# An attention step's order on three engines: key/value projection in three parts, output product behind two heads' scores

## What is computed

```
# attention, for each batch: 32 query heads in 8 groups that share a key/value head, D = 128
q = rope(rmsnorm(x @ Wq.T));  k = rope(rmsnorm(x @ Wk.T));  v = x @ Wv.T
k_all = concat(k_cache[pages], k);  v_all = concat(v_cache[pages], v)      # 512 cached + 128 new keys
probs = softmax(where(valid, q @ k_all.T / sqrt(D), -1e30))
attn  = (probs @ v_all) @ Wo.T
# then
s  = silu(attn @ Wgate.T);  the half of each row of s with the smallest |s| is set to 0
x1 = x + (s * (attn @ Wup.T)) @ Wdown.T
y  = x1 @ W_adapter[id].T;  out = x1 + y @ W_int4.T + b
```

## Time and profile before

| | |
|---|---|
| median of 3 runs | 1438.7 us (1435.5 to 1439.25) |
| the profiled execution | 1440.7 us, span from first to last instruction 1438.9 us |
| TensorE matmul busy | 1397.8 us, 97% |
| TensorE weight load busy | 1167.6 us, 81% |
| VectorE busy | 1178.5 us, 82% |
| ScalarE busy | 871.3 us, 61% |
| GpSimd busy | 803.4 us, 56% |
| mean granted TensorE clock | 0.998 |

### The profile page before, as it was taken

The page is one execution under the profiler, slowest core; times in us unless marked ns, Lnnn a source line. Parts: engine busy times, 40 slices in busy tenths (PEclk is TensorE's granted clock), DMA queues, the critical chain, the costliest instruction groups (busy, mean ns, idle before and its releaser), DMA issues.

```text
span 1438.9 us, 22830 instructions
## 1 busy us (share of the span) xinstructions
PE 1397.8 (97%) x7750; PEld 1167.6 (81%) x7750; DVE 1178.5 (82%) x2596; ACT 871.3 (61%) x2221; POOL 803.4 (56%) x822
## 2 busy tenths in 40 slices
PE   5899999999999999999999999999999999999998
PEld 4788888888888888888888888888888787666766
DVE  7888888888888889888988898889889977666662
ACT  6567666766676767666766676667667751332221
POOL 6566666666666666666666666666666621122211
PEclk9999999999999999999999999999999999999999
DMA  6111211121112111211121111111121303111111
GB/s 221 51 30 29 74 59 32 31 74 59 32 31 74 57 34 30 76 58 32 30 74 60 31 36 68 59 30 52 48 69 32 107 19 116 45 56 62 44 59 52
DMA packets 26767, 80.41 MB, mean 56 GB/s; under 512 B 9522, under 2 KB 10546, under 8 KB 23186
## 3 DMA queue, kind: packets, MB, share of 16 engines
q1 hardware_dynamic: 10258, 45.29, 8.9%
q0 software_dynamic: 16384, 33.59, 8.2%
HBM read 76.74 MB, written 2.10 MB: 55 GB/s over the span
## 4 chain that ended last, share of the span: by engine, by line
PE 86%; DVE 10%; issue 1%; ACT 1%; another core or an unknown queue 0%; DMA 0%; SPq 0%; POOL 0%; DVEq 0%; ACTq 0%
PE proj_ps L108 10%; PE proj_ps L110 9%; PE proj_ps L109 9%; PE turn_ps L712 8%; PE value_ps L108 5%; PE score_ps L108 5%; PE out_ps L877 5%; PE value_ps L110 5%; PE value_ps L109 5%; PE score_ps L110 4%; PE score_ps L109 4%; PE gu_ps L110 3%; PE gu_ps L108 3%; PE gu_ps L109 3%; DVE probs L1437 2%; DVE pt_lo L1462 2%
## 5 line engine op out<-in xcount | busy, mean ns | idle before, releaser
L515 POOL DMA_INDIRECT kg<-kc,idx x256 | 290.1, 1133 | 261.5 <-issue 254.1
L1122 ACT ACTIVATE pt_hi<-turn_ps 128x512 fp32r<-128x512 f32 x320 | 190.2, 595 | 210.2 <-PE turn_ps L712 171.2
L525 POOL DMA_INDIRECT vg<-vc,idx x256 | 251.2, 981 | 109.6 <-issue 58.9
L1462 DVE TENSOR_TENSOR pt_lo<-turn_ps,pt_hi 128x512 fp32r<-128x512 f32 x320 | 218.9, 686 | 66.5 <-ACT pt_hi L1122 49.3
L1116 ACT ACTIVATE probs<-probs,shift,rstd 128x640 f32<-128x640 f32 x256 | 234.0, 916 | 35.4 <-DVE shift L1426 35.4
L1437 DVE CUSTOM_DVE_ANT_0 probs<-score_ps,mask 128x640 f32<-128x640 f32 x256 | 205.4, 817 | 20.2 <-PE score_ps L110 17.9
L108 PE MATMUL proj_ps<-w_hi,xt_hi 128*128 128x512 f32 (+1 forms) x512 | 184.6, 361 | 13.6 <-DVE w_lo L1358 9.8
L712 PE MATMUL turn_ps<-cst,probs 128*128 128x128 f32 x1280 | 191.8, 272 | 0.0
L712 PEld LDWEIGHTS turn_ps<-cst,probs 128*128 128x128 f32 x1280 | 159.8, 140 | 26.4
L108 PE MATMUL score_ps<-kt_hi,qt_hi 128*128 128x320 f32 x512 | 165.1, 323 | 10.5 <-DVE qt_lo L1414 4.4
L110 PE MATMUL proj_ps<-w_hi,xt_lo 128*128 128x512 f32 (+1 forms) x512 | 174.6, 341 | 0.0
(11 more groups left out here) (197 smaller groups left out, 3191.9 us busy)
## 6 DMA issues: line engine op xcount, KB each, us to landing
w_raw<-wqkv SPq DMA_DIRECT2D x7, 1536.0 KB
wo_raw<-wo SPq DMA_DIRECT2D x8, 1024.0 KB
wa_sb<-wa SPq DMA_DIRECT2D x7, 1024.0 KB, 4.9
kg<-kc,idx POOLq DMA_INDIRECT x256
vg<-vc,idx POOLq DMA_INDIRECT x256
wg_raw<-wg SPq DMA_DIRECT2D x2, 1376.0 KB, 5.8
wu_raw<-wu SPq DMA_DIRECT2D x1, 2752.0 KB
wd_sb<-wd SPq DMA_DIRECT2D x1, 2560.0 KB, 9.7
```

The lines of the kernel that those rows point to most:

```text
L515: pool.indirect_dma_start(kg[:, b % 2, c, :], None, kc, bass.IndirectOffsetOnAxis(ap=idx[:, b * NC + c:b * NC + c + 1], axis=0))\
L525: pool.indirect_dma_start(vg[:, b % 2, c, :], None, vc, bass.IndirectOffsetOnAxis(ap=idx[:, b * NC + c:b * NC + c + 1], axis=0))\
L1122: act.activation(pt_hi[:, (b + j) % 2, :], turn_ps[1 - j % 2][:, :], ACT.Copy)\
L1462: dve.tensor_tensor(pt_lo[:, at, :], turn_ps[1 - j % 2][:, :], pt_hi[:, at, :].bitcast(F32), ALU.subtract).then_inc(p_lo_done[j], 1)
```

## The change

The work is the same; the order of the queues of TensorE, ScalarE and VectorE is another.

- TensorE: `project_kv` takes a list of chunks and is called three times: chunk 0 behind the turn of the cached keys, chunk 1 behind the last product with the values, chunks 2 and 3 behind the turn of the new keys. `turn_q` is between the first of them and `values(s, b, 4)`. `values(s, b, 3)` comes behind the last piece of `project_q`. `project_o` comes behind the scores of heads 0 and 1.
- ScalarE: `split_q` and `split_new_k` come before `split_o` and the copies of keys and values; the exponential of head 0 comes before chunk 0 of the next probabilities, from step 0 on.
- VectorE: `split_q` and `split_new_k` come directly behind `split_cached_k`, before `split_o`. The maxima of heads 0 and 1 come before the rotation of the queries and `add_up`. The division of head 0 comes before chunk 3.
- First steps: all eight masks are written before step -2 (before: three there, five in steps 0 to 4). In step -1 the rotation of step 2 and `split_x(4)` come before the maxima. `split_x(3)` goes behind the maxima of step -2.

```diff
-                    def project_kv(s, b, g):
-                        if b == 0:
-                            wait(pe, w_lo_done[2], g + 1)
-                        wait(pe, q_copied, s + 1)
-                        for k in range(NK):
+                    def project_kv(s, b, g, ks):
+                        if ks[0] == 0:
+                            if b == 0:
+                                wait(pe, w_lo_done[2], g + 1)
+                            wait(pe, q_copied, s + 1)
+                        for k in ks:
...
-                        last.then_inc(kv_projected, 1)
+                        if ks[-1] == NK - 1:
+                            last.then_inc(kv_projected, 1)
...
+                        if live(s + 3):
+                            project_q(s + 3, b3, g3, (3,))
                         if live(s):
                             values(s, b, 3)
-                        if live(s + 3):
-                            project_q(s + 3, b3, g3, (3,))
                         if live(s + 2):
                             turn_cached_k(s + 2, b2)
+                        if live(s + 3):
+                            project_kv(s + 3, b3, g3, (0,))
+                        if live(s + 2):
+                            turn_q(s + 2, b2)
                         if s == TAIL + 2:
                             fill(s, 2)
                             front(2)
                         if live(s):
                             values(s, b, 4)
                         if live(s + 3):
-                            project_kv(s + 3, b3, g3)
+                            project_kv(s + 3, b3, g3, (1,))
                         if s == TAIL:
                             front(1)
...
                         if live(s + 2):
-                            turn_q(s + 2, b2)
                             turn_new_k(s + 2)
+                        if live(s + 3):
+                            project_kv(s + 3, b3, g3, (2, 3))
+                        if live(s + 2):
+                            scores(s + 2, (0, 1))
                         if live(s):
                             project_o(s, b, g)
...
-                        if live(s + 2):
-                            scores(s + 2, (0, 1))
                         if live(s + 1):
                             turn_probs(s + 1, b1, 0)
                         if live(s + 2):
...
+                        if s == -1:
+                            split_x(4)
+                        if live(s + 2):
+                            split_q(s + 2)
+                            split_new_k(s + 2)
                         if live(s):
                             split_o(s)
...
-                        if live(s + 2):
-                            split_q(s + 2)
-                            split_new_k(s + 2)
                         if live(s + 3):
                             squares(s + 3)
...
+                        if live(s + 2) and s >= 0:
+                            exps(s + 2, b2, (0,))
+                        if live(s + 1):
+                            split_probs(s + 1, b1, 0)
+                        if live(s + 2) and s < 0:
+                            exps(s + 2, b2, (0,))
...
-                        if live(s + 1):
-                            split_probs(s + 1, b1, 0)
-                        if live(s + 2):
-                            exps(s + 2, b2, (0,))
...
+                        split_x(4)
+                        rotate_q(2, 2)
+                        add_q(2, 2)
                         maxima(1, 1, (0, 1))
                         split_probs(0, 0, 0)
                         maxima(1, 1, (2, 3))
-                        rotate_q(2, 2)
-                        add_q(2, 2)
-                        split_x(4)
...
+                        if live(s + 1):
+                            normalise(s + 1, b1, (0,))
                         if live(s):
                             split_probs(s, b, 3)
...
-                            normalise(s + 1, b1, (0, 1))
+                            normalise(s + 1, b1, (1,))
...
+                        if live(s + 2):
+                            split_q(s + 2)
+                            split_new_k(s + 2)
                         if live(s):
                             split_o(s)
...
-                        if live(s + 3):
+                        if s < 0:
+                            rotate_q(s + 3, s + 3)
+                            add_q(s + 3, s + 3)
+                        if live(s + 2):
+                            maxima(s + 2, b2, (0, 1))
+                        if s >= 0 and live(s + 3):
                             rotate_q(s + 3, (b + 3) % B)
                         if b == B - 4 and live(s + 4):
                             split_w(g + 1, 0)
-                        if live(s + 2):
-                            split_q(s + 2)
-                            split_new_k(s + 2)
-                        if live(s + 3):
+                        if s >= 0 and live(s + 3):
                             add_q(s + 3, (b + 3) % B)
                         split_gate(s, 1)
-                        if -2 <= s < B - 5:
+                        if live(s):
+                            add_up(s, b)
+                        if 0 <= s < B - 5:
                             split_x(s + 5)
-                        if live(s) and s + 3 < B:
-                            hide_keys(s + 3)
                         if s == 0:
                             tables(1, 1)
-                        elif s in (1, 2):
-                            tables(s - 1, 2)
-                        if live(s):
-                            add_up(s, b)
-                        if live(s + 2):
-                            maxima(s + 2, b2, (0, 1))
+                        elif s in (2, 3):
+                            tables(s - 2, 2)
                         if live(s + 1):
                             split_probs(s + 1, b1, 0)
                         if live(s + 2):
                             maxima(s + 2, b2, (2, 3))
+                        if s == -2:
+                            split_x(FIRST)
...
-                    for b in range(FIRST):
+                    for b in range(B):
                         hide_keys(b)
```

2 lines of the change are left out of this document (1 added, 1 removed).

## The result

The changed kernel takes 1442.5 us (median of 8 runs, 1441.0 to 1443.6), the kernel before 1438.3 (8 runs, 1435.5 to 1441.7): ratio 1.0028, interval 1.0017 to 1.0039. Forecast were 1424 us and a range of 1411 to 1435. By the medians the change costs some 4 us where 14 were to be won.

The account below looks back on a forecast made before the run. TensorE, through the starts of its matmuls, was taken to bound the kernel. The terms 8.7 + 2.1 + 0 + 4.1 - 0.6 = 14.3 us, taken from the median 1438.7, gave 1424 us, range 1411 to 1435.

Parts of the forecast that it names:

- Part 5: Step 61: new keys' chain uncovered, 0.6 us lost; maxima and first exponential earlier, rotation later, gathers: 0.
- Part 3: First steps of a head (seven): new keys' turn waits 0.6 or more; costed as 0, bounds minus 1 and plus 4.
- Part 1: TensorE's new order in a step: 0.36 us gained, 0.21 given back to scores' wait; net 0.15 times 58, 8.7 us.
- Part 2: Seven weight steps: the queries' turn rather than chunk 4's product first needs VectorE's late chunk 4; 0.3 each, 2.1 us.
- Part 4: Start, steps 0 to 2: masks ahead, other work behind maxima; 2.2 plus 0.95 each for steps 1 and 2, together 4.1 us.
- rival 2: VectorE's margins fail, scores wait 0.28 to 0.45 and ordinary steps gain nothing: 1433 to 1442, say 1437 us; chance 0.13.
- Rival 3: Queries' part still ahead of new keys' on VectorE, scores wait 0.7, kernel slower: 1457 us; chance 0.06.

Follow-up runs that it names:

- experiment 1: Changed kernel with GpSimd's subtraction for the cached values' low halves left out from step 8 on (result not the block): 1429.7 us, ratio 0.9940 to the kernel before.
- experiment 5: Changed kernel, all work kept, with the split of the values placed earlier in the step on ScalarE and GpSimd: 1425.3 us, ratio 0.9887 to the kernel before.
- run 9: Changed kernel with the values' split early, as in experiment 5, and the old order from step 61 on: 1421.2 us, ratio 0.9887 to the kernel before.
- experiment 6: Changed kernel with ScalarE's first two up-weight copies moved from the end of step 61 to behind step 62's exponentials: 1444.9 us, ratio 1.0025 to the kernel before.
- experiment 7: Changed kernel with the first head's x split and tables spread over steps 1 to 3: 1443.1 us, ratio 1.0014 to the kernel before.

## Why the prediction was wrong

**The step that failed** is the last of Part 5: "nothing on TensorE's path waits for them in an ordinary step, and VectorE's 2.8 us of idle time there cover it: 0." Two things were wrong in it. It was argued for the ordinary step and then taken for 58 steps, and it counted VectorE's time by durations of before, as if an instruction took its time wherever it stands. Six steps with b = 4 (one of three pieces of weights in the same place as rotation and `add_up`) lost 0.57 each against the kernel before instead of winning 0.15; step 4, which has a late chunk 1 besides, lost 1.1. Steps 58 to 60, with the gate weights' split in that place, lost 0.5 to 0.9 each. With b = 0 and b = 1 the hold's 0.7 us over the two ate what the order won. The hold by GpSimd's subtraction is worth 12.8 us (experiment 1, from step 8 on) or 16.5 us of span (experiment 5, the first steps too) in the new order; in the old one it cost nothing visible at b = 4. My sentence "if that cover fails, chunk 1 of the next step is late behind the rotation" named the place. Experiment 5 bears this out: with GpSimd's subtraction out of the way the same order won 10.7 us in steps 3 to 60, nearly all that was forecast there, though not kind by kind (b = 1 won 0.32 and b = 5 0.51, where 0.15 and 0.45 were in the sum). By the spans the forecast was missed by 15.9 us; it would have been 19.8 if the setup had not won 3.9 that were not in the sum, which is luck. What I did not read was a row that was there to be read: `shift`, a 128x1 instruction, 293 ns on average and 1.24 us at b = 4.

The rule is in the Trainium skill, page "SBUF — State Buffer", section "Who interferes with whom": a VectorE instruction with two SBUF inputs contends with a GpSimd instruction that reads SBUF, it is the order of issue that decides who blocks, and one with at most one SBUF input is free unless it runs in a mode that uses both ports. The traces agree: 1.79 for 0.69 (`rot_q`, two SBUF inputs), 1.91 for 1.30 on GpSimd's side when VectorE was first, 0.82 for 0.82 (scores from PSUM, one input from SBUF). By this rule the change speaks against itself, since it exchanges maxima and rotation under GpSimd's subtraction. It would have been a rival with a number. My sum was off in a small thing besides: the seven steps with b = 0 are among the 58 that get 0.15 each, although Part 3 takes them as 0, which is 1.05 us too much.

**Part 1**: mechanism right, sizes near. The ordinary step came to 17.40 (forecast 17.3 to 17.4). Chunk 3's product and the output product, whose late starts are in the earlier trace rows and whose wait is in the earlier trace rows, no longer wait. The scores' wait was 0.19 and its restart 0.07 against 0.13 and 0.08. The steps themselves show 0.11 net instead of 0.15: 26 of the steps from 6 on (b = 2, 3, 6, 7) show it, 3 us in all; the other 32 of the 58 show something else.

**Part 2**: forecast 0.3 each beside the 0.15 of Part 1, measured 0.1 in all (18.99 to 18.91): chunk 1's product starts 0.34 late in them (0.11 before), which is again the late queue of the b = 4 step. Without the hold the same steps took 18.48 (experiment 5), that is 0.5 won.

**Part 3**: taken as 0 within -1 and +4, measured +0.08 for b = 0, on the mean of seven. The reason given is there, the turn of the new keys waits 0.57 (forecast 0.6 or more), but that it came out near 0 is luck in part: without the hold 0.17 was won.

**Part 4**: steps 0 to 2 won 3.5 of 4.1, but not as described. Step 0 gave 2.5 (forecast 2.2), step 2 1.07 (0.95), step 1 nothing: it is rid of the wait for maxima of the earlier trace rows, but the product of chunk 1 starts 1.1 late in it, behind the x split and the tables of step 0. And with the tables of group 2 in steps 2 and 3 the same product starts 1.1 and 0.5 late in steps 3 and 4:

```profile
103.18 0.50 PE L108 MATMUL value_ps<-pt_hi,v_hi 128*128 128x512 f32 x1 [0.85 <-DVE pt_lo L1473]
```

I counted what the change took from steps 1 and 2 and not what it put into 2 and 3. But the tables are the smaller part of it. In experiment 5, where they stand in the same places, the product starts only 0.3 late in step 3 and on time in step 4: ahead of the tables the low half of x was held by GpSimd's subtraction, 1.18 us where it usually takes 0.68.

```profile
97.92 1.18 DVE L1506 TENSOR_TENSOR xt_lo<-x_raw,xt_hi 128x512 fp32r<-128x512 f32 x1
```

The setup, "not priced: 0, give or take 1", gained 3.9; TensorE's wait for the copy of the values fell from 2.21 to 0.54 there, and the one for the queries' low half from 3.66 to 1.89. That ScalarE's copies of the queries no longer stand behind those of keys and values fits, but it wasn't tried by itself.

**Part 5**: step 61 lost 0.8, forecast 0.6. In it the scores wait in the open for the new keys' chain, as described (the trace names `qt_lo`, but the new keys' part on VectorE ended last). The turn's own wait ahead of it is not new, it was 0.71 in the kernel before:

```profile
1146.44 0.33 PE L689 MATMUL turn_ps<-cst,rot_k 128*128 128x128 f32 x1 [0.62 <-DVE kt_lo L1420]
1147.51 0.38 PE L108 MATMUL score_ps<-kt_hi,qt_hi 128*128 128x320 f32 x1 [0.74 <-DVE qt_lo L1425]
```

Step 62 was not in the sum at all and cost 3.7. TensorE waits 2.5 for a low half behind two held `shift`s, and then runs on at half clock for 2 us (below). In the kernel before only the last pair of `shift` was held (3.28), here the one ahead of it too (3.11, then 2.49). That the old order of steps 61 and 62 avoids it, run 9 shows; which of the moved instructions of step 61 sets it stays open, since experiment 6 only exchanged the held instruction for another, and part of the 3.7 varies by itself (step 62 took 19.14 in experiment 7, where nothing was moved near it).

**The rivals.** None of them was this one. The measured 1442.5 lies at the upper end of rival 2's 1433 to 1442, but by another way: the ordinary steps did gain, and the scores waited 0.19, not 0.28 or more. Rival 3 looked for the slower case in the queries' chain, on the instruction that gets a new predecessor. The loss came from instructions that got a new neighbour on another engine.

## What to carry to other kernels

When a hand-written order is rearranged, the duration of a moved instruction is not a constant: before pricing a move, look at what the other engines do at the new place, above all at GpSimd when VectorE reads two tiles of SBUF. A tiny instruction with a mean far over its usual time is a hold at rest; it costs nothing only as long as nothing urgent stands behind it. And an argument made for the ordinary step has to be made again for each kind of step in the count, here the ones that carry an additional piece of weights, the first head's and the last three.
